# Turning g two blocks late and multiplying it down three blocks late in a mixture-of-experts kernel

## What is computed

```python
h   = x @ W_base.T + b_base + low_rank_term(x, cond_8)            # 4096 x 256
top = two best of softmax(h @ gate_w.T), weights made to sum to SCALE
g   = silu(h @ w_gate[e]) * (h @ w_up[e])                          # for the experts e of a token
y   = sum over its two experts of weight * (g @ w_down[e])
s   = (silu(h @ sw_gate) * (h @ sw_up)) @ sw_down                  # shared expert, width 704
out = x + y + s
```

## Time and profile before

| | |
|---|---|
| median of 3 runs | 503.42 us (503.12, 503.42, 508.85) |
| the profiled execution, its own time | 506.99 us |
| its span, first to last instruction | 505.3 us |
| TensorE busy | 490.5 us (97%) |
| VectorE, ScalarE, GpSimd busy | 355.4, 261.1, 249.9 us |
| granted TensorE clock, mean | 0.999 of full speed |

### The profile page before, as it was taken

The page is one execution under the profiler, slowest core; times in us unless marked ns, Lnnn a source line. Parts: engine busy times, 40 slices in busy tenths (PEclk is TensorE's granted clock), DMA queues, the critical chain, the costliest instruction groups (busy, mean ns, idle before and its releaser), DMA issues.

```text
span 505.3 us, 10018 instructions
## 1 busy us (share of the span) xinstructions
PE 490.5 (97%) x3071; PEld 448.2 (89%) x3072; DVE 355.4 (70%) x765; ACT 261.1 (52%) x525; POOL 249.9 (49%) x367
## 2 busy tenths in 40 slices
PE   8999999999999999989999999999999899999996
PEld 7998988888888889988889999999998899888886
DVE  3666778898987556766676677676675666479896
ACT  3567785556663445565455555545554444444322
POOL 2042246655551454666967767677667674211100
PEclk9999999999999999999999999999999999999999
DMA  8387569156222234534344444444444442599942
GB/s 225 130 281 224 169 186 310 57 179 201 45 83 43 84 93 126 119 103 125 104 114 116 114 116 123 123 117 117 112 114 116 115 105 68 145 370 322 384 140 83
DMA packets 104938, 74.54 MB, mean 148 GB/s; under 512 B 61946, under 2 KB 99844, under 8 KB 104900
## 3 DMA queue, kind: packets, MB, share of 16 engines
q1 hardware_dynamic: 95780, 55.21, 37.1%
q0 software_dynamic: 6816, 18.62, 12.5%
q10 hardware_dynamic: 2304, 0.26, 0.5%
HBM read 40.25 MB, written 20.32 MB: 120 GB/s over the span
## 4 chain that ended last, share of the span: by engine, by line
PE 75%; DVE 15%; ACT 5%; issue 4%; DMA 1%; another core or an unknown queue 0%; DVEq 0%; ACTq 0%
PE bank L274 17%; PE bank L276 17%; PE bank L275 17%; PE bank L790 9%; PE bank L762 5%; PE bank L792 5%; DVE bank L1222 2%; ACT gt_h L952 1%; DVE acc L1333 1%; DVE xt_l L1034 1%; ACT x_half L872 1%; DVE x L1058 1%; DVE pos L1081 1%; DMA xin<-in_x_dram 1%; PE bank L576 1%
## 5 line engine op out<-in xcount | busy, mean ns | idle before, releaser
L274 PE MATMUL bank<-w_all,rt_h 128*128 x284 | 97.6, 344 | 0.0
L276 PE MATMUL bank<-w_all,rt_l 128*128 x284 | 91.6, 323 | 0.0
L275 PE MATMUL bank<-w_all,rt_h 128*128 x284 | 91.5, 322 | 0.0
L790 PE MATMUL bank<-w_all,gt_h 128*128 (+1 forms) x213 | 78.0, 396 | 0.2 <-issue 0.2
L551 POOL DMA_INDIRECT y_rows<-y_sb,dst_i x71 | 72.5, 1021 | 11.2 <-POOL spare L465 10.4
L544 POOL DMA_INDIRECT rows<-x_halves,tok_i x71 | 69.5, 978 | 12.5 <-issue 2.2
L952 ACT CAST gt_h<-bank 128x512 fp32r<-128x512 f32 (+1 forms) x48 | 28.1, 586 | 88.7 <-DVE bank L1222 79.8
L274 PE MATMUL bank<-xs_h,sg_h 128*128 128x512 f32 x176 | 70.6, 401 | 0.3 <-DVE gt_h L1233 0.3
L275 PE MATMUL bank<-xs_l,sg_h 128*128 128x512 f32 x176 | 68.9, 391 | 0.0
L276 PE MATMUL bank<-xs_h,sg_l 128*128 128x512 f32 x176 | 68.7, 390 | 0.0
L1295 DVE TENSOR_TENSOR g<-bank,act 128x352 f32<-128x352 f32 x71 | 37.2, 524 | 41.7 <-issue 24.5
(11 more groups left out here) (180 smaller groups left out, 1155.6 us busy)
## 6 DMA issues: line engine op xcount, KB each, us to landing
pick<-y_rows SPq DMA_DIRECT2D x16, 512.0 KB, 7.8
xin<-in_x_dram SPq DMA_DIRECT2D x8, 512.0 KB, 4.8
x_halves<-x_half SPq DMA_DIRECT2D x8, 512.0 KB, 3.3
w_own<-in_L_ffn_w_gate_dram SPq DMA_DIRECT2D x8, 352.0 KB, 4.5
w_own<-in_L_ffn_w_up_dram SPq DMA_DIRECT2D x8, 352.0 KB, 4.7
y_sb<-in_x_dram SPq DMA_DIRECT2D x5, 512.0 KB, 3.5
base_rows<-y_sb SPq DMA_DIRECT2D x5, 512.0 KB, 2.8
acc<-base_rows SPq DMA_DIRECT2D x5, 512.0 KB, 7.1
```

The costliest lines, as they stand in the source:

```text
L274: pe.matmul(o, lh, rh, start=start, stop=False, skip_group_check=skip)
L275: pe.matmul(o, lh, rl, start=False, stop=False, skip_group_check=skip)
L276: return pe.matmul(o, ll, rh, start=False, stop=stop, skip_group_check=skip)
L790: pe.matmul(YE[par][:, 0:2 * D].rearrange("p (h d) -> p h d", h=2), gt_h[par][0:n, cols], both, start=(c == 0), stop=False, skip_group_che ...
```

## The change

`EG`, `EU` and g get a second buffer, `TB` moves to bank 4 (the bank of the shared expert's output, so the first turn waits for group 4's last addition). TensorE's order becomes: gate of block i, turn of g of block i-2, up of block i, down of block i-3. The loop is gone: all 71 blocks are written out, and the expert's number is read at a fixed place. Both `down` of units 28 and 29 come after gate and up of block 0. At the far end, gate (5, 0), turn 69, down 68, up (5, 0), turn 70, gate (5, 1), down 69, down 70, up (5, 1).

ScalarE's and VectorE's lists follow: silu comes before the high half of block i-2, the multiplication before the low half, and `y_sb` is written two blocks later. `y_sb` keeps three of its four tiles for blocks (g's second buffer takes the place of the fourth), and group 4's sums of the shared expert go through `y_last`, in the place of `raw`. The load of group 5's words moves from before the first block's transposing DMA to behind the twelfth; ScalarE's copies of it move from blocks 8 to 13 to blocks 16 to 21; the low half of its split goes from GpSimd (before scatter 14) to VectorE (blocks 20 and 23). GpSimd gathers eight blocks ahead of its scatters, not five.

```diff
-        EG, EU, TB, YE = bank[0], bank[1], bank[2], bank[6:8]
-
-        def known(i, below):
-            return isinstance(i, int) and i < below
+        EG, EU, TB, YE = [bank[0], bank[2]], [bank[1], bank[3]], bank[4], bank[6:8]
...
+                if j == NPG:
+                    sp.wait_ge(s_base, 16 * NPG)
...
-                if j >= 1:
+                if j == NPG - 1:
+                    sp.wait_ge(s_word, 4 * NPG)
+                elif j >= 1:
                     sp.wait_ge(s_base, 16 * j)
...
-                if j + 3 <= NPG:
+                if j + 3 < NPG:
                     load_raw(j + 3, raw)
-            for i in range(4):
+            for i in range(NBLK):
                 turn_rows(i)
-            store_base(NPG - 1)
-            for i in range(4, NBLK):
-                turn_rows(i)
+                if i == 4:
+                    store_base(NPG - 1)
+                if i == 11:
+                    load_raw(NPG, raw)
...
-            for i in range(4):
-                sp.wait_ge(s_sc[i], 16 * ((NBLK - i + 3) // 4))
+            for i in range(N_OUT):
+                sp.wait_ge(s_sc[i], 16 * ((NBLK - i + N_OUT - 1) // N_OUT))
...
-                                        y_sb[:, i % 4, :], None).then_inc(s_sc[i % 4], 16)
+                                        y_sb[:, i % N_OUT, :], None).then_inc(s_sc[i % N_OUT], 16)
...
-            for i in range(5):
+            for i in range(8):
                 gather(i)
             for i in range(NBLK):
-                if i + 5 < NBLK:
-                    gather(i + 5)
-                if i == 14:
-                    split_low(NPG)
+                if i + 8 < NBLK:
+                    gather(i + 8)
                 scatter(i)
...
-            down(*order[NPRE - 2])
...
+            def e_gate(i, e):
+                pe.wait_ge(s_rtl, i + 1)
+
+                if i == 1:
+                    pe.wait_ge(s_gl, UE)
+                else:
+                    pe.wait_ge(s_act, UE + i - 1)
+                e_into(EG[i % 2], i, e, 0, s_G)
+
+            def e_up(i, e):
+                if i < 2:
+                    pe.wait_ge(s_gl, UE - 1 + i)
+                else:
+                    pe.wait_ge(s_g, UE + i - 1)
+                e_into(EU[i % 2], i, e, F, s_U)
+
             def e_turn_g(i):
-                pe.wait_ge(s_g, i + (UE + 1))
+                pe.wait_ge(s_g, UE + i + 1)
+                if i == 0:
+
+                    pe.wait_ge(s_fin, 2 * NPG)
+                else:
+                    pe.wait_ge(s_gl, UE + i)
                 for c in range(FC):
                     n = P if c < FULL else REST
-                    mm = pe.transpose(TB[0:n, c * P:(c + 1) * P], g[:, c * P:c * P + n], ident[:])
+                    mm = pe.transpose(TB[0:n, c * P:(c + 1) * P], g[i % 2][:, c * P:c * P + n], ident[:])
                 mm.then_inc(s_gT_e, 1)
-            def e_gate_up(i, par, e, following):
-
-                pe.wait_ge(s_rtl, i + 1)
-                e_next = e
-                for to, c, ready in ((EG, 0, s_G), (EU, F, s_U)):
...
-            def e_step(i, par, e_prev, e, following):
-                e_turn_g(i - 1)
-                e_next = e_gate_up(i, par, e, following)
-                e_down(i - 1, 1 - par, e_prev)
-                return e_next
-
-            before = expert_of(0)
-            expert = e_gate_up(0, 0, before, 1)
-            down(*order[NPRE - 1])
-            e_step(1, 1, before, expert, None)
-            n_turns = (NBLK - 3) // TURN
-            with pe.Fori(0, n_turns) as q:
-                before = expert_of(q * TURN + 1)
-                expert = expert_of(q * TURN + 2)
-                for s in range(TURN):
-                    before, expert = expert, e_step(
-                        q * TURN + (2 + s), s % 2, before, expert, q * TURN + (3 + s) if s + 1 < TURN else None)
-            i = n_turns * TURN + 2
-            before, expert = expert_of(i - 1), expert_of(i)
-            for n in range(i, NBLK):
-                before, expert = expert, e_step(n, n % 2, before, expert, None if n + 1 == NBLK else n + 1)
-
-
-            e_turn_g(NBLK - 1)
+
+            experts = [expert_of(0)]
+            for i in range(NBLK):
+                e_gate(i, experts[i])
+                if i + 1 < NBLK:
+                    experts.append(expert_of(i + 1))
+                if i >= 2:
+                    e_turn_g(i - 2)
+                e_up(i, experts[i])
+                if i == 0:
+                    down(*order[NPRE - 2])
+                    down(*order[NPRE - 1])
+                if i >= 3:
+                    e_down(i - 3, experts[i - 3])
+
+
             for v, (j, c) in enumerate(order[NPRE:]):
                 gate(j, c)
                 if v >= 2:
                     down(*order[NPRE + v - 2])
                 if v == 0:
-                    e_down(NBLK - 1, (NBLK - 1) % 2, before)
+                    e_turn_g(NBLK - 2)
+                    e_down(NBLK - 3, experts[NBLK - 3])
+                if v == 1:
+                    e_down(NBLK - 2, experts[NBLK - 2])
+                    e_down(NBLK - 1, experts[NBLK - 1])
                 up(j, c)
+                if v == 0:
+                    e_turn_g(NBLK - 1)
             for last in order[-2:]:
                 down(*last)
...
-                sc.activation(act[:, 0:F], EG[:, 0:F], ACT.Silu).then_inc(s_act, 1)
+                sc.activation(act_e[:], EG[i % 2][:, 0:F], ACT.Silu).then_inc(s_act, 1)
...
                 if i + 1 < NBLK:
                     r_word_high(i + 1)
-                e_high(i - 1)
-                if i + 1 < NBLK:
                     r_high(i + 1)
-                if 8 <= i < 14:
-                    k, n = divmod(i - 8, 3)
+                if 16 <= i < 22:
+                    k, n = divmod(i - 16, 3)
                     if n < 2:
                         word(NPG, k, n)
                     else:
                         split_high(NPG, k)
                 e_silu(i)
-            e_high(NBLK - 1)
+                if i >= 2:
+                    e_high(i - 2)
+            e_high(NBLK - 2)
             for u in range(UP, UP + (NG - NPG) * NC):
                 j, c = NPG + (u - UP) // NC, (u - UP) % NC
+                if u == UP:
+
+                    sc.wait_ge(s_gT_e, NBLK)
                 silu(j, c)
+                if u == UP:
+                    e_high(NBLK - 1)
                 g_high(j, c)
                 if c in (1, 2) and j + 1 < NG:
                     split(j + 1, c - 1)
@@ -1250,7 +1284,7 @@
             def base(j):
                 v.wait_ge(s_res, 16 * (j + 1))
-                final(j, y_sb)
...
+
+            def split_low(j, k):
+                b = xs_of(j)
+                v.wait_ge(s_xsh, 2 * j + k + 1)
+                v.tensor_tensor(xs_l[b][:, k, :], xs_w[b][:, k, :], xs_h[b][:, k, :].bitcast(F32), ALU.subtract).then_inc(s_xsl, 1)
+
+            SPLIT_AT = (20, 23)
...
-                if i >= 1:
-                    v.wait_ge(s_gT_e, i)
-                v.tensor_tensor(g[:, 0:F], EU[:, 0:F], act[:, 0:F], ALU.mult).then_inc(s_g, 1)
+                if i >= 2:
+                    v.wait_ge(s_gT_e, i - 1)
+                if i == 1:
+
+                    v.wait_ge(s_base, 16 * (NPG - 1))
+                v.tensor_tensor(g[i % 2][:], EU[i % 2][:, 0:F], act_e[:], ALU.mult).then_inc(s_g, 1)
             def e_low(i):
                 v.wait_ge(s_gh, UE + i + 1)
@@ -1301,28 +1345,32 @@
             def e_y(i):
                 v.wait_ge(s_D, UE + i + 1)
-                if i < 4:
-                    v.wait_ge(s_base, 16 * NPG)
+                if i < N_OUT:
+                    v.wait_ge(s_base, 16 * (NPG - 1))
                 else:
-                    v.wait_ge(s_sc[i % 4], 16 * (i // 4))
-                v.tensor_reduce(y_sb[:, i % 4, :], YE[i % 2][:, 0:2 * D].rearrange("p (h d) -> p d h", h=2), AX.X, ALU.add).then_inc(s_y, 1)
+                    v.wait_ge(s_sc[i % N_OUT], 16 * (i // N_OUT))
+                v.tensor_reduce(y_sb[:, i % N_OUT, :], YE[i % 2][:, 0:2 * D].rearrange("p (h d) -> p d h", h=2), AX.X, ALU.add).then_inc(s_y, 1)
             r_word_low(1)
             r_low(1)
-            e_mul(0)
-            base(NPG - 1)
             for i in range(1, NBLK):
                 if i + 1 < NBLK:
                     r_word_low(i + 1)
-                if i >= 2:
-                    e_y(i - 2)
-                e_low(i - 1)
+                e_mul(i - 1)
                 if i + 1 < NBLK:
                     r_low(i + 1)
-                e_mul(i)
-            e_y(NBLK - 2)
-            e_low(NBLK - 1)
-            e_y(NBLK - 1)
+                if i == 1:
+                    base(NPG - 1)
+                if i in SPLIT_AT:
+                    split_low(NPG, SPLIT_AT.index(i))
+                if i >= 4:
+                    e_y(i - 4)
+                if i >= 2:
+                    e_low(i - 2)
+            e_mul(NBLK - 1)
+            e_y(NBLK - 4)
+            e_low(NBLK - 2)
```

(5 more changed lines are left out.)

61 lines of the change are left out of this document (37 added, 24 removed).

## The result

The changed kernel takes **515.27 us** (median of 514.03, 514.30, 516.25 and 517.09), where 499.8 was forecast in a range of 496.5 to 504.3. Against runs of the kernel before on the same chip (median 505.4) the ratio is 1.0192, with an interval of 1.0113 to 1.0272: 1.1 to 2.7% slower, where a small gain was expected (whether it is more than 2% the interval leaves open). The profiled execution took 516.25 us, 9.3 more than the one before.

What follows compares the result with a forecast made beforehand. TensorE, busy 97% of the span, was taken as the bound, with 10.0 us of idle time recoverable. 506.99 - 10.0 + 1.0 + 2.8 = 500.8 us; leaning on the shorter plain runs gave 499.8, range 496.5 to 504.3.

Steps and rivals of the forecast that it cites:

- The step that failed: Third stage, turn two blocks late: 1.4 us of slack covers late signals of up to 1.9 us; all 10.0 us given back.
- 10.0 to 3.3: Bounds in us of the third stage's gain; 3.3 if none of the 6.7 us idle before the turns comes back.
- Gathers eight ahead keep their distance: GpSimd's list: gathers keep their distance to scatters that come two blocks later; zero, bounds -0.5 and +0.5 us.
- The first turn chain itself: Routed blocks: the turn no longer waits for the multiplication; next late is the low half in `TB`, slack 1.4 us.
- The loop: Routed blocks written out: 12 more instruction fetches, taken as zero; upper bound 1.5 us each.
- The rival that fetches starve TensorE: Written-out blocks: up to 1.5 us for each of 12 fetches, slower, 504 to 518 us; chance 0.07.
- Block 0 ahead of `down`: Start of the routed blocks: TensorE waits 1.0 us for block 0's `rt_l`; bounds 0.8 and 1.2.
- The far end: After the last blocks: sums' loads 3.0 us later, against 0.26 of slack; TensorE loses 2.8 us, bounds 1.5 and 4.0.
- lost time of the array: Third stage: late signals are the array's own lost time, the 6.7 us stay; median 503.9 us, chance 0.15 for 502 to 504.3.
- the rest of the sum: The terms besides the 10.0 us: 1.0 us lost at block 0 and 2.8 us at the far end.

Runs made afterwards that it cites:

- e2: Changed kernel with a second PSUM bank for the turned g, so a turn waits for the subtraction of block i-2; no faster than e4.
- e4: Changed kernel with the down product of the last but one unit back ahead of block 0 and the base rows' loads issued earlier; 24 late stretches, 95 us late.
- e3: Kernel before with its loop of twelve blocks written out, its order, banks and buffers kept; 0.997 of the kernel before.
- e7: Changed kernel with one wait more: the gate product of block i waits for g of block i-1; blocks of 3.60 us in place of 3.31.
- g1: Changed kernel with gate i waiting for g of block i-1, and VectorE's multiplication moved ahead of its copy of the low halves; blocks of 3.38 us.
- g2: Changed kernel with each GpSimd gather replaced by SyncE's plain DMA of 128 neighbouring rows; 0.989 of the kernel before, 68 blocks in 225.17 us.
- h1: Kernel before with each GpSimd gather replaced by SyncE's plain DMA of 128 neighbouring rows; 0.986 of the kernel before, 68 blocks in 226.42 us.
- e6: Changed kernel with the rows of only four blocks gathered and transposed, the other gathers and transposes left out; 0.989 of the kernel before.
- e11: Changed kernel with six gathers only and all 71 transposing DMAs, each waiting for the gate product of block i-2; no late signal, no ratio in the text.
- e1: Changed kernel with TensorE taking each block's expert as a constant, not read into a register; 0.996 of the kernel before.

## Why the prediction was wrong, step by step

**The step that failed** is in the first part of the change: "Late signals of up to 1.9 us are then covered ... I take all 10.0 us as given back". It took the lateness seen in block 9 as a size. It was the size at which TensorE stopped. In the kernel before the chain to the turn has 0.2 us to spare, TensorE stops soon after a signal is late, and the stretches there last 1 to 4 us. With 1.4 us to spare TensorE ran on; stretches were twice as many and reached 5.8 us. On the chip of e2 to e4 it is plainer, in one trace each: five stretches with 0.2 us to spare (e3), 24 with 1.4 (e4), 25 with 1.3 more than that (e2). The stop came all the same, only later, and with two dearer companions: behind the release stood the high and the low half, 1.2 us, where before it was the multiplication, 0.53, and the longer stops were followed by half the clock, 1.57 us each. So the term was not 10.0 to 3.3 but about -4. The bounds failed because both assumed that slack can only help. That slack lets the stretches grow is borne out by e7 and g1, which take it away and have one and two; why a stretch ends when TensorE stops is not shown.

**What made the signals late** was not asked. I went through the queues of GpSimd for their time ("Gathers eight ahead keep their distance ...: zero") and not for what they do to others. g2 and h1 show that the indirect gathers of GpSimd are the cause in both kernels, and e7 and g1 that a wait in each block keeps the stretches few. Whether gathers do it by themselves, or two indirect DMAs in a block where one does not, no run tells apart. g2 and h1 also take scattered rows for neighbouring ones, and drop the small GpSimd instruction (`spare`, L475) ahead of each gather; neither was tried alone. Nor was the way from GpSimd to TensorE's signals found.

**The first turn chain itself** was right: the multiplication no longer stands in front of the turn, ten undisturbed blocks take 33.09 us, and the next late thing is the low half of the block before in the single turn bank, as worked out (its slack, 1.4 us in the sum, is 1.7 in an undisturbed block: the low half ends at 322.00 + 0.56, the next turn starts at 324.25).

**The loop**: zero fits. e3 has its code as long as the changed kernel's and stands at 0.997 (0.993 to 1.001). The rival that fetches starve TensorE had the right sign for the wrong reason. e3 shows no price of straight code. The Trainium skill's rule (Runtime: NRT & Kernel Launch, Instruction fetch mechanics) that straight code is fetched ahead almost for free agrees with e3.

**Block 0 ahead of `down`**: 1.0 us forecast, 1.3 measured, with `rt_l` at 186.16 + 0.42 as what ends last (timeline after):

```profile
186.16 0.42 DVE L1298 TENSOR_TENSOR rt_l<-rt_w,rt_h 128x256 fp32r<-128x256 f32 x1 [0.69 <-ACT rt_h L993]
186.73 0.42 PE L278 MATMUL bank<-w_all,rt_h 128*128 x1 [1.25 <-DVE rt_l L1298]
```

**The far end**: 2.8 us forecast, 3.0 us of idle time more, by the mechanism named. VectorE waits for the picked rows and its low halves are late for two `down`, where before there were 0.26 us to spare:

```profile
457.53 0.38 PE L278 MATMUL bank<-sd_h,gt_h 128*128 128x256 f32 x1 [1.18 <-DVE gt_l L1265]
...
459.43 0.88 DVE L1381 SCALAR_TENSOR_TENSOR acc<-pick,top_w,acc 128x256 f32<-128x256 f32 x2 [0.77 <-DMA pick<-y_rows]
...
462.32 0.38 PE L278 MATMUL bank<-sd_h,gt_h 128*128 128x256 f32 x1 [1.69 <-DVE gt_l L1265]
```

**The rival "lost time of the array"** falls: its time, 503.9, was nearer than mine, but four signals in 0.23 us and 225.17 us for the same products in g2 show that the array had done the work. The Trainium skill (Perfetto Trace Analysis, Tensor Engine Instruction) lets the signal leave when PSUM has acknowledged the writes; no run here shows at which point on that way the signals were held.

With the gathers out of the way the rest of the sum can be set against a measurement: 1.0 + 2.8 us for the two ends, less the 1.25 us by which the 68 blocks are longer in h1 than in g2 (226.42 and 225.17, in part the edges of the loop), is 2.5 us. g2 stands at 0.989 of the kernel before, h1 at 0.986: if anything the change by itself costs 0.3%, some 1.5 us, but the two ran on different chips and their intervals overlap, so a cost is not shown.

## What to carry to other kernels

Before slack is put in front of a stall, ask what ends the stall: if the lateness stops only when the engine does, more slack buys longer stalls. A late signal seen in a tight kernel is cut off by the wait behind it, so its length there is no bound for a looser one. And an engine that nobody waits for can still be the cause: take its work away, or move the same bytes in another way, before the bound of a term is written down.

## What the runs showed of the hardware that was not expected

- Signals of TensorE came up to 4.3 us late (after) while its products went on, and were let out in bursts, four in 0.23 us; stretches lasted 8 us and more (e4). It happened only where GpSimd made indirect gathers beside the routed blocks: e6, e11, g2 and h1, which have at most six of them, show 0 late stretches over 68 blocks each, and in the sixteen traces with 71 gathers no product that starts over 3 us after the last of them has a late signal.
- Within late stretches the releases keep a step: of the intervals between neighbouring releases in six traces (before, after, e1 to e4), bursts aside, 38 are 0.70 to 0.83 us and 46 are 1.40 to 1.58; most of the longer ones lie near 2.2 and 2.9.
- After idle times of TensorE of 2.6 and 2.2 us the granted clock fell from 1.00 to 0.50 for 3.41 us; each time a block took 4.88 us in place of 3.31. e3, whose waits are 1.7 us at most, has one such stretch too (397.69 to 401.10), the kernel before, g2 and h1 have none in the routed blocks.
